# Local attention layers: the score products cut into tiles of 64 rows by 64 columns

## The reference, cut to what matters

```python
for i in range(6):
    x = attn_layer(shift_tokens(x), Wqkv[i], q_scale[i], k_scale[i], Wo[i]) + x
    x = ffn_layer(shift_tokens(x), ln_g[i], ln_b[i], W1[i], b1[i], W2[i], b2[i]) + x
# attn_layer: 16 heads of 64 dimensions; q and k are brought to unit length, scaled and rotated
# local_attention, windows of 32 tokens; a query sees at most the 32 tokens before it and itself
mask = (it < jb) | (it > jb + w) | (jb == -1)
sim = jnp.einsum('bhwie,bhwje->bhwij', bq, bk2) * QK_SCALE
sim = jnp.where(mask, -jnp.finfo(sim.dtype).max, sim)
attn = jax.nn.softmax(sim, -1)
out = jnp.einsum('bhwij,bhwje->bhwie', attn, bv2)
```

## Time and profile before

| | us |
|---|---|
| median of three runs | 5864.9 |
| lowest to highest | 5859.68 to 5867.44 |
| the profiled execution | 5870.52 |
| its span, first to last instruction | 5868.5 |
| first call of `window_layers`, about | 1037 to 3224 |
| second call of `window_layers`, about | 3672 to 5863 |
| mean granted clock of PE | 0.957 |

### The profile page before, as it was taken

One profiled execution on the slowest core, in us unless ns is written; L12 is line 12 of the kernel. 1 busy time (PEld: TensorE's weight loads), 2 busy tenths in 40 slices (PEclk: granted clock), 3 DMA queues, 4 the chain that ended last, 5 costly groups with the idle time before them and its releaser, 6 DMA issues. The chain is left out here.

```text
span 5868.5 us, 157891 instructions
## 1 busy us (share of the span) xinstructions
PE 5444.8 (93%) x59490; PEld 3916.8 (67%) x59490; DVE 4284.4 (73%) x6500; ACT 4035.5 (69%) x7192; POOL 2737.1 (47%) x2483
## 2 busy tenths in 40 slices
PE   8997986899999999999998899899999999999998
PEld 3334442677777777777776333677777777777776
DVE  7876654777777777777775886777777777777775
ACT  5783654677777776777775677677777776777775
POOL 1101100566556666556663110666555656556663
PEclk8996998899999999999999899899999999999999
DMA  0000000100000000000000000100000000000000
GB/s 13 2 2 5 2 3 8 36 17 16 20 14 19 17 16 21 16 17 16 17 20 10 5 2 2 36 17 16 20 14 20 15 16 22 15 17 17 17 19 18
DMA packets 128852, 87.40 MB, mean 15 GB/s; under 512 B 33332, under 2 KB 121936, under 8 KB 128056
## 3 DMA queue, kind: packets, MB, share of 16 engines
q1 hardware_dynamic: 128056, 76.74, 4.6%
HBM read 68.96 MB, written 1.05 MB: 12 GB/s over the span
## 5 line engine op out<-in xcount | busy, mean ns | idle before, releaser
L1737 POOL TENSOR_TENSOR cross<-raw,tab_b 128x512 f32<-128x512 f32 x768 | 997.7, 1324 | 364.4 <-ACT raw L1603 361.6
L737 DVE TENSOR_REDUCE arena<-PS 128x1 f32<-128x512 f32 (+3 forms) x1408 | 828.6, 647 | 217.3 <-PE PS L550 134.2
L1743 POOL CAST kT_b<-kT 128x512 bf16<-128x512 f32 x384 | 253.2, 659 | 1250.1 <-ACT kT L1659 1250.1
L688 ACT ACTIVATE arena<-PS 128x1024 f32<-128x1024 f32 (+1 forms) x704 | 669.0, 968 | 200.1 <-PE PS L573 124.7
L1828 DVE TENSOR_TENSOR rot<-PS,tab_a 128x512 f32<-128x512 f32 x768 | 523.6, 687 | 350.9 <-PE PS L1453 194.1
L1603 ACT COPY raw<-PS 128x512 f32<-128x512 f32 x768 | 447.3, 591 | 352.4 <-PE PS L1453 306.0
L1857 DVE TENSOR_TENSOR oT<-PS,rec_den 128x384 f32<-128x384 f32 (+1 forms) x576 | 299.4, 520 | 457.0 <-ACT rec_den L1637 455.0
L1844 DVE TENSOR_TENSOR rot<-rot,cross 128x1024 f32<-128x1024 f32 x384 | 608.5, 1585 | 15.2 <-POOL cross L1737 15.2
L1408 PE MATMUL PS<-qT,kT 64*128 64x96 f32 x8448 | 613.9, 283 | 0.0
L1851 DVE TENSOR_TENSOR rot<-rot,inv_norm 128x1024 f32<-128x1024 f32 x384 | 583.2, 1519 | 14.2 <-ACT inv_norm L1619 3.7
L1629 ACT ACTIVATE PT<-PS 128x768 f32<-128x768 f32 (+1 forms) x576 | 438.7, 762 | 175.5 <-PE PS L1408 170.7
(11 more groups left out here) (260 smaller groups left out, 13012.4 us busy)
## 6 DMA issues: line engine op xcount, KB each, us to landing
w_qk<-in_w_pairs SPq DMA_DIRECT2D x196, 128.0 KB, 2.1
w_v<-in_w_pairs SPq DMA_DIRECT2D x100, 128.0 KB, 2.2
w_o<-in_w_out_pairs SPq DMA_DIRECT2D x192, 64.0 KB, 1.9
xs<-staged SPq DMA_DIRECT2D x24, 224.0 KB, 2.6
w<-in_L_ffn_W SPq DMA_DIRECT2D x12, 341.0 KB
q_parts<-max_rows SPq DMA_DIRECT2D x192, 2.0 KB
V<-in_c_E SPq DMA_DIRECT2D x2, 896.0 KB, 7.7
w<-in_L_ffn_W SPq DMA_DIRECT2D x24, 64.0 KB
```

What stands on the lines that cost most here:

```text
L688: nc.scalar.activation(PT[u % 6].rearrange("p (a n) -> p a n", a=2)[:, :, first_q:512], PS[:, 2 * (u % 2):2 * (u % 2) + 2, first_q:512], A ...
L737: nc.vector.tensor_reduce(maxima[:, 2 * m + h, qt, kh:kh + 1], bank[:, 0:keys_of(qt, kh)], AX.X, ALU.max).then_inc(bank_free, 1)
L1737: nc.gpsimd.tensor_tensor(dst[:, :, :, o:o + 32], src[:, :, :, other:other + 32], tab[:, :, o:o + 32].unsqueeze(2).broadcast_to([128, 8, 2 ...
```

## The change

Each float32 score product of 64 rows x 128 keys is now two products of 64 rows x 64 keys. The first writes PSUM partitions 0 to 63 (key half w = 0), the second partitions 64 to 127 (w = 1), at tile positions (64h, 64w). The halves are the outer loop and the heads the inner one, so that four products in a row have four different tiles of the array. The masks (L1404), the wait, the semaphore on the last product and all other lines stay as they are.

```diff
                     for i, c in enumerate(chunks):
-                        for h in range(2):
-                            last = nc.tensor.matmul(PS[:, 4 + h, QC * i:QC * i + QC], kT[par][64 * h:64 * h + 64, QC * c:QC * c + 128],
-                                                    qT[par][64 * h:64 * h + 64, QC * c:QC * c + QC], start=False, stop=True,
-                                                    tile_position=(64 * h, 0), skip_group_check=True)
+                        for w in range(2):
+                            for h in range(2):
+                                key = QC * c + 64 * w
+                                last = nc.tensor.matmul(PS[64 * w:64 * w + 64, 4 + h, QC * i:QC * i + QC], kT[par][64 * h:64 * h + 64, key:key + 64],
+                                                        qT[par][64 * h:64 * h + 64, QC * c:QC * c + QC], start=False, stop=True,
+                                                        tile_position=(64 * h, 64 * w), skip_group_check=True)
                     last.then_inc(st_full, 1)
```

## The result

The changed kernel takes 5757.6 us (median of four runs, 5757.2 to 5762.3) against 5865.4 us (5859.7 to 5867.4), a ratio of 0.982, 95% interval 0.9803 to 0.9837. That is 108 us less. The forecast was 5794 us; the range of 5750 to 5835 us holds the result, the forecast's own range of 5778 to 5812 us does not. The profiled execution has a span of 5755.7 us, 112.8 less than the one of before.

A forecast was written before the change was run, and what follows sets the result against it. PE was taken to bound about half the positions alone, taking turns with DVE and ACT elsewhere. 24 x 2.97 = 71 us off 5870.5 gives 5799.5, the median 5.6 lower: 5794 us; own range 5778 to 5812, wide range 5750 to 5835.

The forecast's parts named there:

- What bounds the kernel: Whole kernel: PE, 93% busy, bounds about half of the positions alone; in the others it takes turns with DVE and ACT.
- The load of 128 columns sets 0.112 us, four tiles cost what a pair costs: Score products: the load spaces pairs 0.112 us apart; groups of four take 0.083 us, saving 0.585 us of PE per position.
- The bounds of 0.112 and 0.165 us: Group of four in score products: 0.112 us if loads sharing rows take turns, 0.165 if products sharing rows do.
- The end of a step: End of a score step: the fourth tile starts later than a pair's second, so 0.013 us come back.
- Masks, drains, waits: Around each score step: same shapes before and behind, no wait added or removed, cost nothing.
- What of it reaches the end: Positions 0, 1, 5, 6 keep 0.585 us, the other four 0.157: 2.97 us per batch of a layer, 71 us.
- Each of the four keeps the third step: Positions 2, 3, 4 and 7: waits for DVE or ACT swallow the rest, 0.157 us each is kept.
- all of it counts: Rival, whole kernel: DVE and ACT move along everywhere, all 112 us arrive, 5753 us; chance 0.11.
- its own sign: Whole kernel: wrong on what reaches the end if the step is 0.91 us and the total outside 5778 to 5812.
- positions 3 and 4 would be next: Rival that DVE and ACT take over sooner, being the next bounds in positions 3 and 4: 5829 us; chance 0.14.
- Slower by the clock: Rival, positions 3, 4 and 7: more PE idling brings the lower clock, 122 us lost against 71 gained, 5916; chance 0.04.
- What would show it: Signs in the profile after: four-chunk step 0.91 us, score products busy 502 us, ACT's waits for them some 100 us.

The follow-up runs named there:

- the half-keys run: The changed kernel without the products of the second key half (w = 1), only their mask stays: 5758.4 us, ratio 0.9815.
- the 64-query run: The changed kernel with 64 instead of 96 moving columns in each score product: 5707.9 us, ratio 0.9727.

## Why the prediction was right, and where it was not

- *What bounds the kernel*: right for PE. Where PE's busy time filled the window (positions 0, 5, 6), all of the saving arrived, 0.66 of 0.67 us.
- *The load of 128 columns sets 0.112 us, four tiles cost what a pair costs*: right, and shown by the half-keys run for the width of the operand. Groups 0.0825 us apart were forecast and measured. The bounds of 0.112 and 0.165 us did not come in. In the new step, too, the loads of the second group start 0.055 us after those of the first (single records), while matmuls on the same rows are in flight; the rule of the Trainium skill ("TensorE: Matmul & The Clock Gate", Part 3), by which they would have to wait, disagrees with both traces.
- *The end of a step*: the term that was mis-sized on PE. I booked +0.013 us for the later start of the fourth tile. In fact the last matmul is 0.029 us shorter behind a load of 64 columns, and the next work comes 0.029 us earlier, so that a position gains 0.674 us and not 0.585, 17 us in the kernel. The row was there: I took 0.25 us for the last L1432 and 0.27 for the last L1408 in the same section, and did not use the difference; the part "Masks, drains, waits" puts what follows a step at nothing.
- *What of it reaches the end*: the step that failed. "In positions 2 and 4 the wait is at K0 and q0, behind steps 0 and 1 and ahead of step 2" is wrong: the waits for `rot_done` are at K1, and what swallows the saving in position 4 is the new wait of 0.4 us for the quotients and 0.1 us more for the Gelu. "Each of the four keeps the third step" is wrong in positions 2 and 4 (they keep none) and too little for the rest. 2.97 us per batch of a layer were forecast, 4.07 measured (sum of the medians). Position 3 lost nothing: the waits at L1384 for L1828 are 1.1 us in it and 0.7 us at the start of position 4 in both traces, so they moved along with PE. Their chain runs through ACT's copies, which are under way before Q0 starts, so it is not the case of the earlier trace rows; why it moved was not tested. Per position, 24 x 4.07 = 98 us; by means, which take in the rarer cases, it is 24 x 4.52 = 108. The 10 us between them lie where the granted clock was below 1.00: in the profiled execution before, position 0 was so in 14 of 22 cases and position 3 in 6, after in 10 and 4; against the cases at 1.00 this cost 36.0 and 25.4 us. Whether the change did this is open, since the kernel before alone varies from 5854 us at a mean granted clock of 0.963 to 5877 us at 0.957.
- *The rivals*: "all of it counts" (5753) named the time best, but not the reason: 108 of 129 us arrived, not 112 of 112. The two errors, too small a saving and too small a share, went the same way; that the time still lies within 5750 to 5835 is owed to the width of that range. By its own sign (a step as forecast and a total outside 5778 to 5812) the prediction was right on the products and wrong on what reaches the end. That positions 3 and 4 would be next was right, as the 64-query run shows. *Slower by the clock* did not happen either. But its counter-argument, that positions 3 and 4 keep a clock of 1.00, is true only of the batch that was read: position 3 ran at 0.93 in 6 of 22 cases before the change, 1.5 us longer each, and in 4 after it.
- *What would show it*: the step (0.91 forecast, 0.89 measured), L1410's busy time (502, 484), ACT's waits for it (100, 116.5), the waits for `rot_done` (65, 58.7), the loads shorter by 0.05 us (0.055), positions 2 and 3 shorter by 0.1 to 0.2 us (0.36 and 0.63).
- *Slips in the working*, without effect on the forecast: 8 x 0.06 is 0.48 and not 0.45, and 5778 to 5812 us is 47% to 78% of the 112 us and not 45% to 75%.

## What to carry to other kernels

For a float32 product of few moving columns, compare the distance of its starts with that of a product with equally many moving columns and a narrower load: if the narrower one is closer, the load sets the pace, and cutting the stationary operand into column tiles next to each other in the program costs next to nothing (7.7 us of busy time here). What a faster engine brings is a question of each wait behind it: follow the releaser back, and if it starts from this engine's own earlier work, the wait moves along; if it comes from another step, only savings ahead of that step count. Read more than one batch and sum up more than medians: here the clock of a few positions made 10 of 108 us. A wait that looks like the place where a saving is lost may be worth removing for its own sake, since here moving one DVE instruction ahead brought 54 us before and 28 us after.

## What the runs showed of the hardware that was not expected

- Products for different tiles did not start in the order of the program: with all of w = 0 ahead of w = 1, the marked product of w = 1 started as 15th of 32 although 16 stood ahead, in all 384 steps. Whether the chip or the step from program to instructions does it is open.
- The length of a single float32 matmul follows the stationary's columns: 0.272 us behind 128 columns and 0.243 us behind 64, both with 96 moving columns and 64 rows; with 64 moving columns it is 0.218 us. These ends are modelled, but the start of the next work behind a step moves by the same 0.029 us (0.202 to 0.173) and 0.025 us (0.173 to 0.148).
- Four float32 tiles of 64 x 64 that share rows and PSUM banks cost 7.7 us of busy time over two (484.0 against 476.3 us for all steps), with twice the instructions.
- DVE's second multiplication in a position (128x1024, float32) takes 1.51 us in the mean in both kernels, and with the addition moved ahead of the quotients 1.25 us (1.22 in the kernel before), though the instruction is the same. What shortens it was not tested.
